# A five-layer graph network on one core: four phases by layer, or one loop over graphs

## The reference

```python
# L0 and L3: attention with 12 heads of 32 features
q, k, v = h @ Wq + bq, h @ Wk + bk, h @ Wv + bv
scores = q k^T / sqrt(32)            # L3: / sqrt(384), plus adj
probs = softmax(scores masked by adj > 0)
out = probs @ v                      # L3: then @ Wo + bo
# L1 once, L2 twice: "directed" sublayers
a = softmax(h h^T / sqrt(384)) * adj;  attn = a / (sum(a) + 1e-10)
ctx = upper(attn) @ (h Wl^T + bl) + diag(attn) * (h Ws^T + bs) + lower(attn) @ (h Wr^T + br)
out = relu(layernorm(ctx) * gain + offset)
```

## Time and profile before

| what | us |
|---|---|
| median of 3 runs | 2752.17 (2751.03 to 2753.88) |
| the profiled execution, its own time | 2754.08 |
| its span, first to last instruction | 2752.5 |
| PE busy | 2520.6, 92% |
| DVE busy | 2336.4, 85% |
| ACT busy | 1804.1, 66% |
| POOL busy | 1453.0, 53% |
| mean granted TensorE clock | 0.979 of full |

### The profile page before, as it was taken

How to read it: one execution, slowest core, us unless ns; L and a number is a source line. 1 busy time by engine, 2 the same in 40 slices (tenths; PEclk the granted TensorE clock), 3 DMA queues, 4 the chain that set the end, 5 groups by cost and what they waited for, 6 DMA issues and landing times. The chain is left out here.

```text
span 2752.5 us, 86859 instructions
## 1 busy us (share of the span) xinstructions
PE 2520.6 (92%) x27969; PEld 1884.4 (68%) x27969; DVE 2336.4 (85%) x9515; ACT 1804.1 (66%) x4409; POOL 1453.0 (53%) x2016
## 2 busy tenths in 40 slices
PE   5999999986999999699999999999969999999998
PEld 4888888874666665466666666666648888888886
DVE  5778777776999999688888888888859999999997
ACT  5888888874555555455555555555538777777775
POOL 1233232324777777477777777777734434444443
PEclk9999999997999999799999999999979999999998
DMA  3011010102000000100000000000000000000000
GB/s 105 28 30 29 28 30 27 30 14 88 9 9 10 10 10 9 46 10 10 10 10 10 10 10 10 10 10 10 10 6 22 24 25 23 27 23 27 23 27 23
DMA packets 73988, 60.19 MB, mean 22 GB/s; under 512 B 7888, under 2 KB 73936, under 8 KB 73936
## 3 DMA queue, kind: packets, MB, share of 16 engines
q1 hardware_dynamic: 73936, 59.54, 7.1%
HBM read 46.92 MB, written 12.58 MB: 22 GB/s over the span
## 5 line engine op out<-in xcount | busy, mean ns | idle before, releaser
L149 PE MATMUL bank<-L_w_hi,L_hT_hi 128*128 128x384 f16 x2112 | 691.7, 327 | 0.0
L151 PE MATMUL bank<-L_w_hi,L_hT_lo 128*128 128x384 f16 x2112 | 691.5, 327 | 0.0
L150 PE MATMUL bank<-L_w_lo,L_hT_hi 128*128 128x384 f16 x2112 | 691.4, 327 | 0.0
L550 ACT ACTIVATE raw_weights<-L_minus_scores,L_minus_max 128x128 f32<-128x128 f32 x1536 | 476.0, 389 | 69.5 <-DVE L_minus_max L665 67.7
L149 PE MATMUL bank<-L_hT_hi,L_w_hi 128*128 128x128 f16 x2304 | 413.4, 220 | 1.7 <-issue 1.2
L150 PE MATMUL bank<-L_hT_lo,L_w_hi 128*128 128x128 f16 x2304 | 413.3, 220 | 0.0
L151 PE MATMUL bank<-L_hT_hi,L_w_lo 128*128 128x128 f16 x2304 | 413.2, 220 | 0.0
L665 DVE CUSTOM_DVE_ANT_0 L_minus_scores<-bank,L_minus_score_bias 128x128 f32<-128x128 f32 x1536 | 347.8, 282 | 11.4 <-PE bank L834 5.9
L692 DVE TENSOR_TENSOR L_pT_lo<-bank,L_pT_hi 128x512 f16<-128x512 f32 x384 | 241.0, 682 | 126.6 <-ACT L_pT_hi L572 126.5
L1069 ACT ACTIVATE L_e<-bank,L_nmax 128x128 f32<-128x128 f32 x192 | 70.6, 368 | 365.6 <-DVE L_nmax L1154 365.6
L151 PEld LDWEIGHTS bank<-L_w_hi,L_hT_lo 128*128 128x128 f16 x2112 | 207.5, 98 | 138.2 <-issue 2.5
(11 more groups left out here) (165 smaller groups left out, 7531.3 us busy)
## 6 DMA issues: line engine op xcount, KB each, us to landing
adj_tile<-in_adj SPq DMA_DIRECT2D x320, 64.0 KB, 1.8
x<-in_x SPq DMA_DIRECT2D x64, 192.0 KB, 2.3
out<-L_result SPq DMA_DIRECT2D x64, 192.0 KB, 1.9
raw_weights<-in_L_gnn_Wq SPq DMA_DIRECT2D x2, 576.0 KB, 4.0
raw_weights<-in_L_gnn_Wk SPq DMA_DIRECT2D x2, 576.0 KB, 5.7
raw_weights<-in_L_gnn_Wv SPq DMA_DIRECT2D x2, 576.0 KB, 5.5
raw_weights<-in_L_gnn_Wl SPq DMA_DIRECT2D x2, 576.0 KB, 4.9
raw_weights<-in_L_gnn_Ws SPq DMA_DIRECT2D x2, 576.0 KB, 4.8
```

Of the source, the lines that this page charges most:

```text
L149: pe.matmul(out, stat[0], move[0], start=first, stop=False)
L150: pe.matmul(out, stat[0], move[1], start=False, stop=False)
L151: return pe.matmul(out, stat[1], move[0], start=False, stop=last)
L550: last = act.activation(probs[:, n_.slot(k), i, :], scores[:, i, :], ACT.Exp, bias=nmax[:, n_.slot(k), i:i + 1], scale=-1.0)
```

## The change

The four phases become one loop over rounds. `Round n` has, on each engine, parts of five tasks: L3 of graph n-2 (`last(2)`), the two sublayers of L2 of graph n-1 (`upper(1)` is the second one) and of graph n (`lower(0)`), L1 of graph n (`single(0)`) and L0 of graph n+1 (`first(-1)`). The lags are such that a graph's layers follow one another from round to round. Rounds run from -2 to 66; rounds 4 to 61 are the hardware loop, two to an iteration. In rounds 2 to 62 all five layers are at work. Every engine has one `step`, a written-out list in which the five tasks' parts are mixed.

All weights stay in SBUF, split, in 16 places (`w_hi`, `w_lo`). L0's are prepared at the start, those of L1, L2 and L3 one set after the other ahead of round 0 (`more_weights`), in which the raw area is used again, so W2 is loaded when W1 is ready and W3 when W2 is. To make room, `x` is no longer kept: each layer hands it on in two slots (`x0` to `x3`), and small tiles lie in the raw area afterwards.

The turn of `probs` leaves PE. ACT and DVE split the f32 `probs` in SBUF into `p16` (`probs_hi`, `probs_lo`), and SP issues a transposing DMA for each third of the heads, 128 x 1024 f16 elements (256 KB), from `p16` to `pT`, that PE's `attend` waits for, a third at a time.

The PSUM banks are dealt out anew: three are shared by a directed task's products, one by the attention's outputs, four by the turned h, q, k, v and the scores.

The core of the diff:

```diff
-                        def turn_probs(n_, k, c):
-                            wait(pe, probs_ready[c], n_.done(k))
-                            for j in range(HC):
-                                mm = pe.transpose(pT_banks[c][:, c128(j)], probs[:, n_.slot(k), HC * c + j, :], ident[:, :])
-                            mm.then_inc(pT_psum[c], 1)
...
-                            dve.tensor_tensor(pT[1][:, hs, :], pT_banks[c][:, :].rearrange("p (h q) -> p h q", h=HC),
-                                              pT[0][:, hs, :], ALU.subtract).then_inc(pT_lo[c], 1)
...
+                def probs_hi(t, c):
+                    if t is None:
+                        return
+                    wait_apart(act, (probs_ready[c], t.count()), (pT_ready[c], t.count(-1, 16)))
+                    act.activation(p16[:, c, 0, :, :], probs[:, HC * c:HC * c + HC, :], ACT.Copy).then_inc(p_hi[c], 1)
...
+                def probs_lo(t, c):
+                    if t is None:
+                        return
+                    wait(dve, p_hi[c], t.count())
+                    dve.tensor_tensor(p16[:, c, 1, :, :], probs[:, HC * c:HC * c + HC, :], p16[:, c, 0, :, :],
+                                      ALU.subtract).then_inc(p_lo[c], 1)
...
+                def turn_probs(t, c):
+                    if t is None:
+                        return
+                    wait_apart(sp, (pT_ready[c], t.count(-1, 16)), (p_lo[c], t.count()), (pv_psum, t.count(-1)))
+                    sp.dma_start_transpose(pT[:, c, :, :],
+                                           p16[:, c, :, :, :].rearrange("p a h n -> p (a h n)")).then_inc(pT_ready[c], 16)
...
+def run_rounds(eng, step, before_round):
+
+    for n in range(FIRST_ROUND, LOOP[0]):
+        if n in before_round:
+            before_round[n](eng)
+        step(Round(eng, n))
+    with eng.Fori(LOOP[0] // 2, LOOP[1] // 2) as i:
+        values = {"i": i, "from": LOOP[0] // 2}
+        for s in (0, 1):
+            step(Round(eng, (2, s), values))
...
+                def more_weights(eng):
+                    W0.ready(sp)
+                    W1.ready(sp)
+                    W2.load(sp)
+                    W2.ready(sp)
+                    W3.load(sp)
+                    W3.ready(sp)
```

More of the change, by code:

```diff
@@ L62, in _value @@
         a, b = v
+        if a * self.values["from"] + b < 1:
+            raise ValueError("a count under one in the loop")
         if v not in self.values:
@@ L115, with count @@
-class TwoLayerPhase(Phase):
-    tasks = 2 * G
-    def kind_of(self, t):
-        if isinstance(t, int):
-            return "first" if t == 0 or (t % 2 and t < self.tasks - 1) else "second"
-        return "first" if t[1] % 2 else "second"
-    def graph_of(self, t):
-        if isinstance(t, int):
-            return t // 2 + t % 2 if self.kind_of(t) == "first" else (t - 1) // 2 if t % 2 else t // 2 - 1
-        return (1, (t[1] + 1) // 2) if t[1] % 2 else (1, t[1] // 2 - 1)
-    def run(self, eng, step):
-        for t in range(self.first):
-            step(Turn(eng, self, t))
-        with eng.Fori(self.first // 2 + 1, G - 1) as i:
-            values = {"i": i}
-            step(Turn(eng, self, (2, -1), values))
-            step(Turn(eng, self, (2, 0), values))
-        for t in range(self.tasks - self.last, self.tasks + self.after):
-            step(Turn(eng, self, t))
+    def count(self, k=0, each=1, of=None):
+        p = self.order.before(self.kind, self.graph, self.order.kinds if of is None else of)
+        if isinstance(p, int):
+            return (p + k + 1) * each
+        return self._value((p[0] * each, (p[1] + k + 1) * each))
@@ L140, in wait @@
+def run_rounds(eng, step, before_round):
[7 more added lines that the diff above has]
+            step(Round(eng, (2, s), values))
+    for n in range(LOOP[1], LAST_ROUND + 1):
+        step(Round(eng, n))
 def wait(eng, sem, value):
@@ new lines, in __init__ @@
+                self.to_load += [(self.raw_bias[:, k], src.partition_broadcast(P)) for k, src in enumerate(biases)]
+                self.to_load += [(dst, src.partition_broadcast(P)) for dst, src in straight]
+                self.n_prepared, self.n_turned, self.n_split = (self.count[k] for k in ("phases", "turned", "split"))
+                self.bias_before = self.count["bias"]
+                self.loaded = sem(f"weights_loaded_{self.n_prepared}")
+                self.count["phases"] += 1
@@ new lines, in __init__, with scales @@
+                self.count["split"] += len(self.work)
+                self.count["turned"] += len(self.work) if transposed else 0
+                self.count["bias"] += sum(len(bs) > 0 for _, bs in groups)
+                self.count["kept"] += keeps
+                self.count["kept_by_pool"] += keeps_of_pool
+                self.all_kept_by_pool = self.count["kept_by_pool"]
+                self.all_split, self.all_kept = self.count["split"], self.count["kept"]
+            def scales(self, g):
+                return scale[:, self.column + g:self.column + g + 1]
```

2193 lines of the change are left out of this document (1160 added, 1033 removed).

## The result

The changed kernel takes 2947.68 us (median of 4 runs, 2946.28 to 2953.51) against 2752.78 for the kernel before: 1.0713 times the time, interval 1.0694 to 1.0731. The forecast was 2673, with 2550 to 2840 as the range. It is slower, and by more than the range allows.

What follows compares the result with a forecast made beforehand. DVE was taken to bound the rounds, closely ahead of PE: 61 full rounds of 38.7 us plus 312 us of head and tail gave 2673 us, range 2550 to 2840.

Steps and rivals of the forecast that it cites:

- In-order engines never mesh fully: Full rounds: the bounding engine, DVE at 37.5 us, was taken as 97% busy, giving 38.7 us per round.
- rings of waits bound it, which I have not priced: Unpriced case for the rounds, to be shown by a clock below 1.00 or PE and DVE both idle by 10%.
- the slower cases: Two rivals: late transposing transfers, 2831 us, chance 0.19; more DVE waits for POOL, 2819 us, chance 0.14.
- PE's work: PE's own work per round, with the probabilities' turns and some weight turns removed: 36.4 us.
- DVE's work and the port: DVE per round: 33.1 us of work plus 4.4 us of waiting for POOL's running operations, 37.5 us together.
- low bound: DVE's waits for POOL if met as rarely as before: 0.142 us per operation, 3.4 us per round.
- shared port: Rival: all 30 DVE operations meet POOL at random, 6.8 us, a round of 41.1 us, 2819 us; chance 0.14.
- The transfer: Transposing DMA of 256 KB from SBUF to `pT`, taken to land in 3 us, range 1.8 to 8.2.
- hidden up to 2.9: For `first`, a transfer of up to 2.9 us is covered; above, each microsecond stops DVE at `row_sums(first)`.
- A sound part by itself: Expectation for e6: DMA turns alone gain up to 84 us in L0, 0 to 30 in L3; best guess 2680.
- PE bounds: Rival: waits for POOL stay cheap, PE at 98% sets a round of 37.2 us, 2581 us; chance 0.20.
- Head and tail: Time outside the 61 full rounds: 166 us ahead plus 146 us of partial rounds, 312 us together.

Runs made afterwards that it cites:

- e5: Changed kernel without hardware loop, step orders chosen anew by an estimate including DVE-POOL exclusion, late transfers and longer hops: 2672.4 us, 0.9701 of the kernel before.
- e9: The orders of e5 with the changed kernel's hardware loop of two rounds put back: 2878.5 us, 1.0462 of the kernel before.
- e2: Changed kernel with one DVE operation, a low part of the probabilities of `last`, moved behind the context's statistics: 2918.9 us, 1.0604 of the kernel before.
- e8: Changed kernel with denominator and `scaled_eps` written as DVE operations with one SBUF input: 2923.1 us, 1.0615 of the kernel before.
- e3: Changed kernel, loop kept, with other step orders found by an estimate using the prices of its own trace alone: 2939.1 us, 1.0678 of the kernel before.
- e7: Changed kernel with each transposing transfer made twice and PE waiting for both: 3230.8 us, 1.1739 of the kernel before.
- e6: Kernel before, phases and loops unchanged, with the probabilities split in SBUF and turned by DMA instead of PE: 3032.4 us, 1.1020 of the kernel before.
- e10: As e5, with the orders chosen once more, starting from e5's and using its durations: 2667.8 us, 0.9696 of the kernel before.
- e4: Changed kernel without hardware loop, with other step orders found using the prices of the changed kernel's trace alone: 2898.5 us, 1.0528 of the kernel before.
- e1: Changed kernel without the hardware loop, all rounds written out in the same orders: 2907.0 us, 1.0558 of the kernel before.
- run 275: Not a run's label: 275 counts the packets of 16 KB of instructions fetched in the changed kernel's whole run, which takes 2947.68 us.

## Why the prediction was wrong

**The step that failed** is "In-order engines never mesh fully: the bounding one reached 95.5% and 98.2%, and I take 97%". These rows come from phases in which one or two kinds of task repeat. With five tasks in one round the ring through PE, ACT, DVE and POOL set the period: PE reached 86.7 and DVE 82.6%, and a full round took 42.9 us instead of 38.7. That it was the orders, e5 shows: the same work in other orders has rounds of 38.5 us. Which piece of the ring costs how much stays open. The prediction named this in its last lines, "rings of waits bound it, which I have not priced", with the sign that came true (PE and DVE both idle by 10%), and had folded it into the slower cases, whose upper end of 2840 was worked out without it. It should have been a rival with a place and a price. The signals were there: four engines whose orders hand on to one another 17 times on the way through a round, each time with a hop (in this trace 0.03 us from ACT to DVE, 0.14 from ACT to PE) and whatever stands ahead in the queue.

**The jump of a long loop body** was not in the sum at all. Nothing in the trace of before priced it for so long a body; that kernel fetches 0.44 MB of instructions in all on this queue, this one 4.51. The loop costs 41 us here, 206 in e9.

**PE's work:** forecast 36.4 us per round; busy in the middle 0.867 x 42.9 = 37.2, and in e5 0.948 x 38.5 = 36.5. Right within some 2%.

**DVE's work and the port:** the mechanism was right, the size too high. The five groups above, against 682, 551, 150, 148 and 209 ns where they don't meet POOL, waited 35 + 50 + 29 + 16 + 12 = 142 us, 2.2 us per round, where 4.4 were taken and 3.4 was the low bound. So it isn't what made the kernel slow by its sum, and the rival "shared port" fell as it was priced. Nor is it what e5 won back by its sum. e2 and e8 gain 29 and 25 us, about what DVE's durations lose. That `mask` and `diagonal` belong to the operations that wait, which I had left open, e3 shows (347 and 667 ns against 291 and 284). Here the Trainium skill ("Advanced Engine Details and Errata", GPSIMD Details) had told that DVE's instructions with two SBUF inputs conflict with POOL over a shared interface, and these two traces agree. One case doesn't go by it: DVE's `left_lo` that starts during POOL's power of [128,1] takes 550 ns, as alone.

**The transfer:** 3 us taken, 2.8 measured, and PE waited for it 16.6 us in all. The turning point, "hidden up to 2.9", and the slope behind it, one microsecond of a round for each microsecond, fit e7: the third that the prediction called tight lands 3.7 us later, and a round takes 4.1 us more. "A sound part by itself", which I expected of it in e6, is wrong: alone it makes a phase of one layer slower, since no other layer's work covers 2.8 us.

**"PE bounds"**, the rival at 37.2 us per round, tells which engine sets the floor: e5 and e10 reach 38.5 and 38.4 with PE at 94 to 95%, and DVE in e5 is at 89%.

**The forecast itself**, 2673 us, is what e5 takes, 2672.4. That is luck and doesn't make it right: in e5 PE bounds and not DVE, and a round is 0.2 us shorter and head and tail 16 us longer than forecast, so that two errors cancel. About this time the work takes when its orders mesh, and I took for granted that they did.

**Head and tail:** 312 forecast, 328 found, with two errors that partly cancel. DVE begins round 0 at 144.2 us, where 166 was forecast. The six partial rounds take 75 us ahead of round 2 and 109 behind round 62, 184 in all, where 146 were taken.

## What to carry to other kernels

When several kinds of task are interleaved in hand-written orders, the sum of an engine's work is a floor and not a forecast: follow the trace back over several rounds and see through which engines the way goes, then move what stands ahead of the ring's members in each queue. Choose orders with every price in them; with some missing (the port's exclusion, late transfers, longer hops) the same search gained 9 us on the orders given (e4 against e1), with them 235 (e5). Which of the prices mattered most, no run shows. Keep a long loop body from jumping often, since each engine stops at its own moment; and put a transfer of some microseconds only where other work covers it, with slack.

## What the runs showed of the hardware

- DVE's operations with two SBUF inputs (or scaling several elements from SBUF to SBUF) and POOL's wide ones exclude one another, in both directions: in e4 `left_lo` goes from 0.55 to 2.05 us behind POOL's 1.82, POOL's L627 from 0.91 to 1.36 behind `probs_lo`. POOL's [128,1] products wait as well (L605, 0.19 to 0.40 us beside `left_lo` in the changed kernel).
- With POOL's power of [128,1] it goes one way only. It waits for DVE: in the changed kernel 62 of 192 (L612) start while `probs_lo` runs and take 0.93 us instead of 0.55, ending 0.41 us after it. DVE doesn't wait for it: 63 `left_lo` that start during a power take 550 ns, where 61 that start during other work of POOL take 1374 (medians). One such power, and the low part ahead of it:

```profile
1623.39 0.68 DVE L955 TENSOR_TENSOR p<-probs,p 128x512 f16<-128x512 f32 x1
1623.55 0.93 POOL L612 TENSOR_TENSOR cln_scale_bias<-cvar_eps,minus_half 128x1 f32<-128x1 f32 x1 [0.66 <-DVE cvar_eps L1164]
```

- A jump back of a body of two rounds stops PE for 2.0 to 4.6 us and DVE for 2.6 to 2.7 (changed kernel, e3, e9). In the whole run 275 packets of 16 KB of instructions are fetched, 4.51 MB. With all rounds written out (e1) it is 3.49 MB, and PE and DVE have no such stops.
- A transposing transfer of 128 x 1024 16-bit elements from SBUF to SBUF lands in 2.8 us (median; 3.1 in e6) and keeps SP 1.24 us. It comes late beside instruction packets: of the changed kernel's 292 issued from 500 to 2600 us, three quarters of the 196 with no such packet beside them landed within 2.77 us, three quarters of the 96 with one within 3.35, and in e4 some took 5.3. That the packets are the cause is likely, but only this coincidence is shown.
- PE's granted clock fell to the lower level for a while at stops of 3 to 4.6 us (mean 0.95 in e3, 0.97 in e9), in e3 as often behind a few waits of 1 us close together. It was 0.99 on average where the same work ran with stops of 2 us (changed kernel) or none (e5).
